# A mixture-of-experts stage that computes its inner rows transposed and streams its up weights per tile

## What is computed

```
gout = xt @ Wg.T                              # 4096 rows, 8 experts
topv, topi = top_k(gout, 2);  w = softmax(topv)
g = einsum('th,efh->etf', xt, W1) + b1        # per expert, 128 -> 256
v = einsum('th,efh->etf', xt, W2) + b2        # per expert, 128 -> 256
h = silu(g) * v
eo = einsum('etf,ehf->eth', h, W3) + b3       # 256 -> 128
out = sum of the two chosen experts' eo, weighted by w
x = layernorm(x + out)
```

## Time and profile before

| | before |
|---|---|
| device time, median of 3 runs | 1457.57 us (1446.95, 1458.02, 1457.57) |
| profiled execution, device time | 1453.48 us |
| its span, first to last instruction | 1451.7 us |
| first up matmul of the m0 stage | 689.7 us into the span |
| last addition into y of the m0 stage | 811.3 us into the span |
| busy over the whole span: PE, DVE, ACT, POOL | 83%, 74%, 58%, 37% |

### The profile page before, as it was taken

One profiled execution on the slowest core, in us unless ns is written; L12 is line 12 of the kernel. 1 busy time (PEld: TensorE's weight loads), 2 busy tenths in 40 slices (PEclk: granted clock), 3 DMA queues, 4 the chain that ended last, 5 costly groups with the idle time before them and its releaser, 6 DMA issues. The chain is left out here.

```text
span 1451.7 us, 31640 instructions
## 1 busy us (share of the span) xinstructions
PE 1207.3 (83%) x9948; PEld 806.1 (56%) x9948; DVE 1076.9 (74%) x3184; ACT 845.2 (58%) x2331; POOL 534.8 (37%) x798
## 2 busy tenths in 40 slices
PE   3889999999999999872999689999997899859900
PEld 2556666666666656541666355555554777637700
DVE  3578888888888888764788599999997466456644
ACT  2678878787878788641566256666665344333300
POOL 1233324344444444424000465655531146510065
PEclk9999999999999999985999799999999599779965
DMA  7100000000000000001222223130000001112133
GB/s 275 28 13 14 16 16 27 20 25 22 23 23 22 22 16 14 14 10 57 69 84 82 58 98 125 40 94 23 22 5 1 6 24 41 36 59 59 50 92 90
DMA packets 84815, 65.88 MB, mean 45 GB/s; under 512 B 11440, under 2 KB 79792, under 8 KB 83760
## 3 DMA queue, kind: packets, MB, share of 16 engines
q1 hardware_dynamic: 73856, 47.18, 10.5%
q0 software_dynamic: 6144, 12.60, 2.6%
q10 hardware_dynamic: 4656, 4.10, 0.9%
HBM read 40.76 MB, written 23.07 MB: 44 GB/s over the span
## 5 line engine op out<-in xcount | busy, mean ns | idle before, releaser
L693 PE MATMUL e_bank_turned<-c_matrices,e_probs 128*128 128x128 f32 x1024 | 165.0, 285 | 17.2 <-ACT e_probs_t L925 9.8
L925 ACT ACTIVATE e_probs_t<-e_bank_turned 128x512 f32<-128x512 f32 x256 | 154.8, 605 | 16.6 <-PE e_bank_turned L693 14.9
L629 POOL TENSOR_TENSOR e_rstd<-e_var_eps,c_minus_half 128x1 f32<-128x1 f32 x128 | 71.1, 576 | 250.6 <-DVE e_var_eps L961 250.3
L1047 DVE TENSOR_REDUCE e_neg_max<-e_bank_scores 128x4 f32<-128x512 f32 x160 | 109.6, 685 | 49.2 <-PE e_bank_scores L736 48.6
L693 PEld LDWEIGHTS e_bank_turned<-c_matrices,e_probs 128*128 128x128 f32 x1024 | 115.9, 144 | 40.8 <-issue 17.0
L703 PE MATMUL e_bank_mix<-e_probs_t,e_values 128*32 128x128 f32 x2048 | 111.5, 291 | 15.7 <-ACT e_probs_t L925 15.4
L884 ACT ACTIVATE e_probs<-e_scores,e_neg_max 128x128 f32<-128x128 f32 x384 | 123.3, 410 | 1.1 <-DVE e_neg_max L1083 1.1
L1249 PE MATMUL m_wide<-up,m_rowsT 128*128 x224 | 119.0, 614 | 0.5 <-ACT m_rowsT L1313 0.4
L1657 ACT ACTIVATE d_probs_t<-d_bank_turned 128x512 f32<-128x512 f32 x128 | 77.3, 604 | 62.7 <-PE d_bank_turned L1542 62.6
L1290 DVE TENSOR_TENSOR m_pre<-m_wide,up_b 128x512 f32<-128x512 f32 x112 | 77.3, 690 | 43.9 <-PE m_wide L1249 42.8
L879 ACT ACTIVATE e_probs<-e_scores 128x512 f32<-128x512 f32 x128 | 82.1, 641 | 42.1 <-DVE e_scores L1080 41.6
(11 more groups left out here) (310 smaller groups left out, 3139.1 us busy)
## 6 DMA issues: line engine op xcount, KB each, us to landing
m_rows<-scratch_sorted SPq DMA_DIRECT2D x112, 64.0 KB, 1.7
scratch_expert_out<-m_y SPq DMA_DIRECT2D x112, 64.0 KB, 1.5
e_x_in<-in_x SPq DMA_DIRECT2D x32, 64.0 KB, 1.8
e_ctx_in<-in_ctx SPq DMA_DIRECT2D x32, 64.0 KB, 2.1
up<-in_m_wgv SPq DMA_DIRECT2D x1, 2048.0 KB, 7.6
up_b<-in_m_bgv SPq DMA_DIRECT2D x1, 2048.0 KB, 14.1
scratch_ctxT<-e_xT_ctxT SPq DMA_DIRECT2D x32, 64.0 KB, 1.6
scratch_x<-e_x SPq DMA_DIRECT2D x32, 64.0 KB, 1.7
```

The lines of the kernel that those rows point to most:

```text
L693: last = nc.tensor.transpose(turned_bank[:, j * P:(j + 1) * P], pr[k % 3][:, j, :], c["ident"][:])
L925: nc.scalar.activation(pt[k % 2][:], turned_bank[:], ACT.Copy).then_inc(probs_t_ready, 1)
L1047: nc.vector.tensor_reduce(nmax[k % 4][:], bank, AX.X, ALU.max, negate=True).then_inc(max_ready, 1)
```

## The change

A new function `phase_gated` takes the place of `phase_experts` for m0. The first two matrices and the two biases of an expert are laid out by the host side as one block `m_up` of 128 partitions by 516 floats (264 KB), in columns: W1 transposed (256), W2 transposed (256), b1 in two columns, b2 in two columns.

- Every tile loads the block of its own expert by a DMA of SP into a ring `up` of 5 (`UPS0`), once tile n-5 has left it. The resident `up` and `up_b` of the first stage and their loads in the encode phase go away.
- PE multiplies with the weights as the stationary side and `rowsT` as the moving side: four matmuls of 128 columns, each giving 128 inner features by 128 rows. The result is already transposed, so the two transposes of `h` go away.
- Features now lie along partitions, so a bias is one value per partition. ACT takes b1 as the bias of its Silu, two instructions of 128x128 read from the matmul's result. DVE computes (v + b2)·gate in two instructions of 128x128. The addition over 512 columns, the product `h` and the copy of ACT to `hT` go away.
- SP issues, for each n: rows of n+8, the up block of n+5, the y of n-1. It now loads registers from two tables. Down and y come one tick earlier than before (n-2).

The wait counts on `experts_loaded` are lowered to fit.

```diff
--- before.py
+++ after.py
@@ -605,7 +605,7 @@
             for n in range(4):
                 load(n)
             sp.wait_ge(act_written, ACT_TURNS["x_x1_mix1", -2] + 1)
-            load_experts(sp, keep, experts0, d, ("m_wgv", "m_wd", "m_bgv", "m_bd"))
+            load_experts(sp, keep, experts0, d, ("", "m_wd", "", "m_bd"), (1, 3))
             for tick in ENCODE_TICKS:
                 if (n := at(tick, -8)) is not None:
                     sp.wait_ge(act_read, ACT_TURNS["x_x1_mix1", n - 2] + 1)
@@ -1161,20 +1161,160 @@
-def expert_buffers(nc, ctx, tag, down):
+def expert_buffers(nc, ctx, tag, down, up=True):
     def sb(name, shape):
         return ctx.enter_context(nc.sbuf_tensor(name + tag, shape, F32))
-    return dict(up=sb("up", [P, EXPERTS, FF1]), up_b=sb("up_b", [P, EXPERTS, FF1]),
-                 down=sb("down", [P, EXPERTS, down, P]), down_b=sb("down_b", [P, EXPERTS, P]))
+    resident = dict(up=sb("up", [P, EXPERTS, FF1]), up_b=sb("up_b", [P, EXPERTS, FF1])) if up else {}
+    return dict(down=sb("down", [P, EXPERTS, down, P]), down_b=sb("down_b", [P, EXPERTS, P]), **resident)
 def load_experts(sp, keep, e, d, names, parts=(0, 1, 2, 3)):
     up, down, up_b, down_b = names
     for part in parts:
-        tile, src = ((e["up"], d[up]), (e["down"], d[down]), (e["up_b"], d[up_b].partition_broadcast(P)),
-                     (e["down_b"], d[down_b].partition_broadcast(P)))[part]
-        sp.dma_start(tile[:], src).then_inc(keep["experts_loaded"], 16)
+        tile = e[("up", "down", "up_b", "down_b")[part]]
+        src = d[(up, down, up_b, down_b)[part]]
+        sp.dma_start(tile[:], src if part < 2 else src.partition_broadcast(P)).then_inc(keep["experts_loaded"], 16)
+ROWS_AHEAD0, UPS0 = 8, 5
+BLOCKS0 = FF0 // P
+def phase_gated(nc, c, d, keep, kept, e, sorted_rows, out_rows, loaded):
+    with Phase(nc) as ctx:
...
+        rows, rowsT, up = sb("rows", [P, P], ROWS_AHEAD0), sb("rowsT", [P, P]), sb("up", [P, FF1 + 2 * BLOCKS0], UPS0)
+        gateT, hT, y = sb("gateT", [P, FF0]), sb("hT", [P, FF0]), sb("y", [P, P])
...
+        TICKS = range(-2, tiles + 3)
...
+        @block.sync
+        def _(sp):
+            row_of, expert_of = loader(sp, "row", "tile_row", EXPERTS * REGION - P), loader(sp, "in", "tile_expert", EXPERTS - 1)
+            for n in range(-ROWS_AHEAD0, tiles):
+                k = n + ROWS_AHEAD0
+                if k < tiles:
+                    if k % SLOTS == 0:
+                        at_rows = row_of(k // SLOTS)
+                    if k >= ROWS_AHEAD0:
+                        sp.wait_ge(rows_transposed, k - ROWS_AHEAD0 + 1)
+                    sp.dma_start(rows[k % ROWS_AHEAD0][:], sorted_rows[bass.ds(at_rows[k % SLOTS], P), :])\
+                        .then_inc(rows_loaded[k % ROWS_AHEAD0], 16)
+                k = n + UPS0
+                if 0 <= k < tiles:
+                    if k % SLOTS == 0:
+                        experts = expert_of(k // SLOTS)
+                    if k >= UPS0:
+                        sp.wait_ge(hT_ready, k - UPS0 + 1)
+                    sp.dma_start(up[k % UPS0][:], dram_tile(d["m_up"], experts[k % SLOTS])).then_inc(up_loaded[k % UPS0], 16)
+                k = n - 1
+                if k >= 0:
+                    sp.wait_ge(y_ready, k + 1)
+                    sp.dma_start(out_rows[k * P:(k + 1) * P, :], y[k % SLOTS][:]).then_inc(y_saved[k % SLOTS], 16)
...
+        @block.tensor
+        def _(pe):
+            expert_of = loader(pe, "down", "tile_expert", EXPERTS - 1)
+            pe.wait_ge(keep["experts_loaded"], loaded)
+            for tick in TICKS:
+                if 0 <= (n := tick) < tiles:
+                    pe.wait_ge(rowsT_ready, n + 1)
+                    pe.wait_ge(up_loaded[n % UPS0], 16 * (n // UPS0 + 1))
+                    if n >= SLOTS:
+                        pe.wait_ge(hT_ready, n - SLOTS + 1)
+                    for k in range(2 * BLOCKS0):
+                        last = nc.tensor.matmul(wide[n % SLOTS][:, k * P:(k + 1) * P], lhsT=up[n % UPS0][:, k * P:(k + 1) * P],
+                                                rhs=rowsT[n % SLOTS][:], start=True, stop=True)
+                    last.then_inc(up_done, 1)
+                if 0 <= (n := tick + 2) < tiles:
+                    pe.wait_ge(rows_loaded[n % ROWS_AHEAD0], 16 * (n // ROWS_AHEAD0 + 1))
+                    if n >= 2:
+                        pe.wait_ge(rowsT_ready, n - 1)
+                    nc.tensor.transpose(turned_rows[n % 2][:, 0:P], rows[n % ROWS_AHEAD0][:], c["ident"][:]).then_inc(rows_transposed, 1)
+                if 0 <= (n := tick - 2) < tiles:
+                    if n % SLOTS == 0:
+                        experts = expert_of(n // SLOTS)
+                    pe.wait_ge(hT_ready, n + 1)
+                    if n >= 2:
+                        pe.wait_ge(y_ready, n - 1)
+                    for k in range(BLOCKS0):
+                        last = nc.tensor.matmul(
+                            sums[n % 2][:, 0:P], lhsT=hT[n % SLOTS][:, k * P:(k + 1) * P],
+                            rhs=e["down"][:, bass.ds(experts[n % SLOTS], 1), k, :].rearrange("p o n -> p (o n)"),
+                            start=k == 0, stop=k == BLOCKS0 - 1)
+                    last.then_inc(down_done, 1)
+        @block.vector
+        def _(dve):
+            expert_of = loader(dve, "bias", "tile_expert", EXPERTS - 1)
+            dve.wait_ge(keep["experts_loaded"], loaded)
+            for tick in TICKS:
+                if 0 <= (n := tick) < tiles:
+                    dve.wait_ge(gate_ready, n + 1)
+                    if n >= SLOTS:
+                        dve.wait_ge(down_done, n - SLOTS + 1)
+                    for k in range(BLOCKS0):
+                        block_k = slice(k * P, (k + 1) * P)
+                        last = nc.vector.scalar_tensor_tensor(
+                            out=hT[n % SLOTS][:, block_k], in0=wide[n % SLOTS][:, FF0 + k * P:FF0 + (k + 1) * P],
+                            scalar=up[n % UPS0][:, FF1 + BLOCKS0 + k:FF1 + BLOCKS0 + k + 1], in1=gateT[n % SLOTS][:, block_k],
+                            op0=ALU.add, op1=ALU.mult)
+                    last.then_inc(hT_ready, 1)
+                if 0 <= (n := tick - 2) < tiles:
+                    if n % SLOTS == 0:
+                        experts = expert_of(n // SLOTS)
+                    dve.wait_ge(down_done, n + 1)
+                    if n >= SLOTS:
+                        dve.wait_ge(y_saved[n % SLOTS], 16 * (n // SLOTS))
+                    nc.vector.tensor_tensor(y[n % SLOTS][:], sums[n % 2][:, 0:P], tile_of(e["down_b"], experts[n % SLOTS]), ALU.add)\
+                        .then_inc(y_ready, 1)
+        @block.scalar
+        def _(act):
+            for tick in TICKS:
+                if 0 <= (n := tick) < tiles:
+                    act.wait_ge(up_done, n + 1)
+                    if n >= SLOTS:
+                        act.wait_ge(hT_ready, n - SLOTS + 1)
+                    for k in range(BLOCKS0):
+                        last = nc.scalar.activation(gateT[n % SLOTS][:, k * P:(k + 1) * P], wide[n % SLOTS][:, k * P:(k + 1) * P],
+                                                    ACT.Silu, bias=up[n % UPS0][:, FF1 + k:FF1 + k + 1])
+                    last.then_inc(gate_ready, 1)
+                if 0 <= (n := tick + 2) < tiles:
+                    act.wait_ge(rows_transposed, n + 1)
+                    if n >= SLOTS:
+                        act.wait_ge(up_done, n - SLOTS + 1)
+                    nc.scalar.activation(rowsT[n % SLOTS][:], turned_rows[n % 2][:, 0:P], ACT.Copy).then_inc(rowsT_ready, 1)
 AHEAD = 8
@@ -2203,8 +2343,8 @@
         x_wo=con(f["L0_xattn_Wo"].T), x_bq=f["L0_xattn_bq"], x_bk=f["L0_xattn_bk"], x_bv=f["L0_xattn_bv"],
         x_bo=f["L0_xattn_bo"], gate0=con(f["L0_ffn_Wg"].T),
-        m_wgv=con(np.concatenate([f["L0_ffn_W1"], f["L0_ffn_W2"]], axis=1).transpose(2, 0, 1)),
-        m_bgv=con(np.concatenate([f["L0_ffn_b1"], f["L0_ffn_b2"]], axis=1)),
+        m_up=con(np.concatenate([f["L0_ffn_W1"].transpose(0, 2, 1), f["L0_ffn_W2"].transpose(0, 2, 1)] + [
+            f[k].reshape(EXPERTS, FF0 // P, P).transpose(0, 2, 1) for k in ("L0_ffn_b1", "L0_ffn_b2")], axis=2)),
         m_wd=f["L0_ffn_W3"].transpose(2, 0, 1).reshape(FF0 // P, P, EXPERTS, P).transpose(1, 2, 0, 3), m_bd=f["L0_ffn_b3"],
         l_wq=con(qkv[:, 0:P]), l_wk=con(qkv[:, P:2 * P]), l_wv=con(qkv[:, 2 * P:]),
         l_wqp=con(qkv[:, 0:P][:, swap]), l_wkp=con(qkv[:, P:2 * P][:, swap]),
@@ -2250,16 +2390,16 @@
         keep, scr = keep_buffers(nc, ctx), scratch(nc)
         c = load_constants(nc, ctx, d)
         with ExitStack() as first:
-            experts0 = expert_buffers(nc, first, "0", FF0 // P)
+            experts0 = expert_buffers(nc, first, "0", FF0 // P, up=False)
             phase_encode(nc, c, d, scr, keep, experts0)
-            phase_experts(nc, c, keep, keep["route0"], experts0, "m0", True, scr["sorted0"], scr["expert_out0"], 16 * 4)
```

(37 more changed lines are left out.)

## The result

| | before | after |
|---|---|---|
| device time, median | 1455.80 us (4 runs, 1446.95 to 1458.02) | 1474.46 us (4 runs, 1473.42 to 1475.59) |
| profiled execution, device time / span | 1453.48 / 1451.7 us | 1475.36 / 1473.6 us |
| m0 stage, first row load issued to end of the last y addition | 125.0 us (686.5 to 811.6) | 140.6 us (687.8 to 828.3) |

The changed kernel is slower: ratio 1.014, 95% interval 1.0095 to 1.0185, or 18.7 us between the medians. The forecast was 1463, inside a range up to 1475; the time lies at that range's upper edge and the loss is more than twice what was foreseen.

What follows compares the result with a forecast made beforehand. SP's issue time was taken to bound the m0 stage at 1.75 us a tile; +3.4 us summed along SP's queue and 4.4 for long issues made +7.8, giving 1461.3 to 1465.4, taken as 1463 us, range 1446 to 1475.

Steps and rivals of the forecast that it cites:

- PE's side: m0 stage: PE's tile falls from 1.63 to 1.46 us; if PE stays the bound, 72 tiles give −12.6 us.
- DVE and ACT: m0 stage: DVE 0.99 us and ACT about 1.0 us a tile, beside PE's 1.46; costed at nothing.
- SP's pace: m0 stage: three issues 1.51 us plus 0.24 for register loads, 1.75 us a tile, above PE's 1.46.
- rival B: m0 stage: PE stays the bound at 1.46 us a tile, SP's issues fit under it; 1446 us, chance 0.15.
- +3.4: m0 stage: last y addition at 814.7 us in place of 811.3, from summing SP's issues, landing and final chain.
- +4.4: m0 stage: SP's long issues, one in 40 of 216 with 0.8 us excess, 4.4 us; bounds 0 and twice that.
- The encode side: Encode phase, near 21 to 40 us: 4 MB less moved, costed at 0; gain up to 2 us not excluded.
- The translation to a median: Whole kernel: profiled execution plus 7.8 gives 1461.3 us, with the median 4.1 above it 1465.4; 1463 was taken.
- 392 KB a tile: m0 stage: bytes moved per tile, 128 KB plus 264 KB, taking the DMA engines 0.99 to 1.43 us; costed at nothing.
- C: m0 stage: an up issue is dearer than a row load; at 2.0 us a tile 1481 us, chance 0.17.
- D: m0 stage: landing over 5.5 us outruns the ring of 5; at 7.6 us, 2.2 a tile and 1493, chance 0.06.
- one in 40 issues: m0 stage: share of SP's issues that run long, 0.94 to 1.30 us in place of 0.33, excess 0.8 us.

Runs made afterwards that it cites:

- experiment 1: Changed kernel with the m0 stage's y stores issued by ACT in place of SP: stage 117.3 us, kernel 1451.79 us against 1456.48 for the kernel before, ratio 0.9953.
- experiment 2: Changed kernel with a ring of 8 up blocks in place of 5, nothing else: m0 stage 141.5 us against 140.6.
- experiment 3: Changed kernel loading only 260 of 516 columns of each up block, same instructions: m0 stage 139.5 us against 140.6.
- experiment 5: Kernel before plus the changed kernel's up loads and register loads, into an unread spare ring: stage 142.2 us, kernel 1470.54 against 1451.42, ratio 1.0132.
- the second profile: The changed kernel, unchanged, profiled again: m0 stage 143.0 us against 140.6, whole span 1469.3 us against 1473.6.
- experiment 8: Changed kernel, ring of 8, y stores on ACT: 1443.06 us against 1453.42 before, ratio 0.9926; or on GpSimd with the last 8 on SP: 1442.79, ratio 0.9921.

## Why the prediction was right in kind and wrong in size

**PE's side: right.** Up passes 0.112 apart, a tile of 1.45 us where nothing holds it back (forecast 1.46), and 14.2 us less stage without the loads (forecast 12.6).

**DVE and ACT: right.** DVE's two instructions measured 0.346 us, ACT's 0.364; both engines stay far from the pace.

**SP's pace: right to 0.01 us for a plain tile.** 1.51 us was summed and 1.51 is measured; a register load was 0.47 and is 0.47. That SP takes over as the bound, and that PE then waits, was the forecast, and experiments 1, 2, 3 and 5 agree, each against a rival. The Trainium skill's rule (DMA: Bandwidth & Descriptors, section "Issuing engines are not separate DMA queues") that the time to start a transfer is usually small beside the transfer was cited for rival B's 1446. Here one start is 0.52 us beside a landing of 3.3, about a sixth, and still starts set the pace: the transfers of several tiles overlap, the starts of one queue do not, and three of them with the registers take 1.75 us a tile where PE takes 1.45. Moving one of the three elsewhere gained 23 us. Where the same section says that issuing from several engines saves just that start-up time, the runs agree: here it was all there was to save.

**The step that failed is the sum from there to the end of the stage**, +3.4 and +4.4 where 15.5 was measured. The mechanism was right; its terms for the long issues, the register loads, the first waits and the end were too small, 7.7 us together. Term by term, in the first profile:

- First row load to last up issue: 122.6 + 4.4 forecast, 687.8 to 819.9 = 132.1 measured, 5.1 more (in the second profile 134.3, 7.3 more). Of this, the first y was waited for 2.1 us, not 1.1, and an up load waited 0.6 for `hT` during the fill, where I had no wait. Nine long issues (0.66 to 1.45 us) have an excess over 0.33 of about 5.8 us together where 4.4 was put. The rate had been taken from three issues of before's stage, but there was a fourth, the longest:

```profile
789.35 1.76 SPq L1234 DMA_DIRECT2D scratch_expert_out<-m_y  x1
```

  With it the same rule, 4 in 144 with an excess of 3.9 us together, gives 5.8 for 216 issues. That it then meets the measured value is in part luck, since the long issues do not come with the count of issues (last section). The loads of registers for the up table took 2.0 us more than 0.47 each: four of the 18 were 0.34 to 0.46 longer, those before the blocks of tiles 12, 28, 44 and 60, the same four in both profiles, and six more by 0.04 to 0.16. One of the four is here:

```profile
710.14 0.33 SPq L1227 DMA_DIRECT2D m_rows<-scratch_sorted  x1
711.59 0.34 SPq L1235 DMA_DIRECT2D m_up<-in_m_up  x1
```

  1.45 us against 0.99 above. The two waits, the long issues and the register loads make 5.0 of the 5.1 us.

- Last up issue to the start of the last y addition: 5.6 forecast, 8.2 measured, 2.6 more. The landing was taken as 2.2 us, from the lone 64 KB load and the rate of the large ones; it is 3.3. And I let the last tile run through an empty PE. But when SP has no more rows to load, it issues up loads 1.0 us apart, faster than PE's 1.45, and PE falls behind at the very end (SP, then PE):

```profile
816.86 0.33 SPq L1235 DMA_DIRECT2D m_up<-in_m_up  x1
...
817.85 0.33 SPq L1235 DMA_DIRECT2D m_up<-in_m_up  x1
...
818.88 0.33 SPq L1235 DMA_DIRECT2D m_up<-in_m_up  x1
...
819.88 0.33 SPq L1235 DMA_DIRECT2D m_up<-in_m_up  x1
```

```profile
821.61 1.06 PE L1256 MATMUL m_wide<-m_rowsT,m_up 128*128 128x128 f32 x8
...
823.06 1.06 PE L1256 MATMUL m_wide<-m_rowsT,m_up 128*128 128x128 f32 x8
...
824.40 1.06 PE L1256 MATMUL m_wide<-m_rowsT,m_up 128*128 128x128 f32 x8
```

  Tile 71's block had landed by 823.2 and its matmuls start at 824.40. So 1.1 us of the 2.6 are landing and 1.2 are the wait for PE; the way from there to the y took 3.65 us where 3.4 was put.

**The encode side: right at 0.** The stage begins 1.3 us later in one profile of after and 0.6 later in the other, within what before's two profiles differ by (686.5 and 687.9).

**The translation to a median was too hopeful.** I put the median at 1463 by averaging two bases, and the chance of a loss over 1% at 0.24. All error terms (a wait, a landing, a stall) could only lengthen a chain that I had found to have no slack; yet I took small readings of the wait and the landing, put half of the range below the sum, and lowered the median again by mixing the bases. The forecast's 392 KB a tile are a slip too: 264 and 131 are 395 thousand bytes, which makes its bounds 0.98 to 1.41 us and changes nothing.

**The rivals.** B was wrong as long as SP has three issues. With two its mechanism came true, PE at 1.50 us a tile (experiment 1) and at 1.45 (experiment 8). C (an up issue dearer than a row load) did not hold: 0.33 for both, median over 72, and half the bytes left the long issues as they were (11, excess 7.6 us, in experiment 3). D did not hold (experiment 2), though its 5.5 us of allowed landing was closer to the measured 2.8 to 4.7 than I thought (5.4 once in the second profile).

## What to carry to other kernels

Before a change adds a transfer per tile, add up its queue as if it were a compute engine: distances of issues that come without a wait, plus the register loads, against the tile time of the engine that binds now and of the one that will. A queue that shows long waits may be one transfer a tile from being the bound (here it waited 51 us in 72 tiles, and one issue more with its registers put it over), and once it is, every stall of it counts in full, at the fill and the end too. Then look for an idle queue to take one of the issues before giving the change up, and deepen the ring only after that.

## What was not expected of the hardware

- **The DMA engines are nearly full in the best version.** With the stores on ACT and a ring of 8 they are busy 0.95 of the time at 278 GB/s, 0.95 × 1.45 = 1.38 us a tile, near the poor end of the forecast's 0.99 to 1.43. But for the same bytes it was 0.81 × 1.88 = 1.52 us a tile in the changed kernel, so this busy time is no fixed price of the bytes. That a further cut of PE's work would meet the DMA engines as the next bound is likely and not shown.
- **Long issues.** In the m0 stage of the changed kernel 9 of SP's 209 issues up to the last up load take 0.66 to 1.45 us in place of 0.33; before's stage has 4 of 144 over 0.9. The one at 720.54 falls together with a 16 KB piece of the instruction queue (the DMA queues from 720.1 to 721.9 us: packets, MB, share of 16 engines):

```profile
q1 hardware_dynamic: 361, 0.35, 73.9%
q8 instruction: 1, 0.02, 4.9%
```

  This holds for all of them. In the m0 stages of the thirteen profiles 109 of SP's row, up and y issues take 0.55 us or more, and during each of the 109 a packet of an instruction queue (q8 or q14) is in flight; of the other 2203 issues that is so for 170. There are 16 to 20 such packets in every stage, whatever SP issues. The kernels with the stores elsewhere have 144 to 152 issues on SP and 8 or 9 long ones (excess 5.8 to 7.7 us), the changed kernel has 216 and 9 or 10 (5.8 and 8.0), before 144 and 4 or 5 (3.9 and 2.3). So the forecast's rule, one in 40 issues, does not hold. No run took the instruction traffic away, so that it causes them is likely and not shown.
- **Same program, other pace.** All that lies outside the m0 stage took 1324.7 to 1333.3 us together in thirteen profiles, in steps (313 or 316 in the decode phase, 13.4 to 14.0 or 15.4 to 15.6 before m1), with the same kernel on both steps. Differences under 9 us between single profiles of this program say nothing unless they are cut by stage.
